# Softmax denominators in a windowed-attention feed-forward: a copy between SBUF tensors in place of a trip through DRAM, and another order of tasks

## What is computed

```
x = x + 0.5 * ffn(layernorm(x))
x = x + attn(layernorm(x))
x = x + 0.5 * ffn(layernorm(x))
```

```
for l in range(2):
    q, k, v = split(shift_token(x) @ wqkv[l])           # 8 heads of 64
    q = l2norm(q) * q_scale[l];  k = l2norm(k) * k_scale[l]
    q, k = rotary_xpos(q, k)
    o = softmax(mask(8 * q @ k.T)) @ v                  # own window and the one before
    x = x + o @ wo[l]
    h = layernorm(shift_token(x)) * ln_g[l] + ln_b[l]
    a, g = split(h @ w1[l] + b1[l])
    x = x + (a * gelu(g)) @ w2[l] + b2[l]
```

## Time and profile before

| | us |
|---|---|
| median of 3 runs | 2139.76 (2129.42 to 2140.91) |
| the profiled execution: its own time | 2146.62 |
| its span, from the first to the last instruction | 2144.8 |
| TensorE busy | 1746.9 (81%) |
| VectorE busy | 1369.1 (64%) |
| GpSimd busy | 979.3 (46%) |
| ScalarE busy | 938.8 (44%) |

### The profile page before, as it was taken

One profiled execution on the slowest core, in us unless ns is written; L12 is line 12 of the kernel. 1 busy time (PEld: TensorE's weight loads), 2 busy tenths in 40 slices (PEclk: granted clock), 3 DMA queues, 4 the chain that ended last, 5 costly groups with the idle time before them and its releaser, 6 DMA issues. The chain is left out here.

```text
span 2144.8 us, 48275 instructions
## 1 busy us (share of the span) xinstructions
PE 1746.9 (81%) x19914; PEld 1024.5 (48%) x19914; DVE 1369.1 (64%) x2002; ACT 938.8 (44%) x1503; POOL 979.3 (46%) x692
## 2 busy tenths in 40 slices
PE   1578888888888887799999997678888888888885
PEld 1345444545545544455555553344444555555543
DVE  2466777666776664456666654577777776666752
ACT  1134444544445443245555554234444544544532
POOL 2444455455455451444444441445445545445530
PEclk9888999999999999589999998799999999999998
DMA  4333343455343452000000000243444534355441
GB/s 143 37 58 63 68 73 64 74 77 86 63 78 63 79 75 50 12 1 2 1 2 1 1 1 1 37 73 63 64 77 73 86 65 76 63 85 86 85 78 36
DMA packets 66060, 118.94 MB, mean 55 GB/s; under 512 B 13183, under 2 KB 23603, under 8 KB 63667
## 3 DMA queue, kind: packets, MB, share of 16 engines
q1 hardware_dynamic: 65843, 115.85, 32.1%
HBM read 49.61 MB, written 3.28 MB: 25 GB/s over the span
## 5 line engine op out<-in xcount | busy, mean ns | idle before, releaser
L953 POOL TENSOR_TENSOR QK<-QK,RB 128x1024 f32<-128x1024 f32 x128 | 302.2, 2361 | 120.2 <-DMA RB<-RN 120.2
L793 DVE SCALAR_TENSOR_TENSOR TP<-banks,cols,tab 128x1024 f32<-128x1024 f32 x256 | 318.3, 1274 | 52.5 <-PE banks L457 46.5
L947 POOL TENSOR_TENSOR QK<-TP 128x512 f32<-128x512 f32 x128 | 164.7, 1287 | 332.0 <-DVE TP L793 288.8
L1315 DVE TENSOR_REDUCE NM<-banks 128x2 f32<-128x1024 f32 (+3 forms) x256 | 202.9, 820 | 129.4 <-PE banks L1128 129.4
L1244 ACT ACTIVATE PTL<-banks 128x1024 f32<-128x1024 f32 (+1 forms) x192 | 168.1, 884 | 192.9 <-PE banks L1159 190.5
L816 DVE TRANSPOSE_TENSOR_REDUCE MX<-banks 128x16 f32<-128x512 f32 x256 | 160.2, 682 | 122.3 <-PE banks L494 122.3
L649 ACT ACTIVATE SQ<-banks 128x512 f32<-128x512 f32 x128 | 76.6, 599 | 279.1 <-PE banks L457 278.8
L834 DVE TENSOR_TENSOR OT<-banks,OT 128x512 f32<-128x512 f32 x128 | 85.3, 687 | 158.6 <-DMA OT<-sums_d 143.9
L939 POOL TENSOR_TENSOR HTL<-Z,HTH 128x512 fp32r<-128x512 f32 x32 | 37.8, 1182 | 303.8 <-ACT HTH L643 303.8
L457 PE MATMUL banks<-HTH,wqkv_h 128*128 128x512 f32 x256 | 125.3, 490 | 54.4 <-DVE TP L793 43.2
L655 ACT ACTIVATE SQ<-banks 128x512 f32<-128x512 f32 x128 | 76.7, 599 | 200.3 <-DVE TP L793 200.3
(11 more groups left out here) (182 smaller groups left out, 3636.0 us busy)
## 6 DMA issues: line engine op xcount, KB each, us to landing
RB<-RN SPq DMA_DIRECT2D x512, 64.0 KB, 4.0
OT<-sums_d SPq DMA_DIRECT2D x128, 256.0 KB, 4.0
V<-V SPq DMA_DIRECT2D x32, 512.0 KB, 6.0
V<-V SPq DMA_DIRECT2D x32, 384.0 KB, 7.1
RB<-vars_d SPq DMA_DIRECT2D x32, 256.0 KB, 3.3
X<-in_L_attn_x SPq DMA_DIRECT2D x8, 256.0 KB, 4.5
out<-X SPq DMA_DIRECT2D x8, 256.0 KB, 4.6
wqkv_raw<-in_L_ffn_wqkv SPq DMA_DIRECT2D x1, 1536.0 KB
```

What stands on the lines that cost most here:

```text
L793: nc.vector.scalar_tensor_tensor(out=TP[:, o:o + 2, :], in0=BK[4 + z][:, :].unsqueeze(1).to_broadcast([P, 2, T]), scalar=q, in1=tab[:, e, ...
L947: nc.gpsimd.tensor_tensor(QK[:, m, 0, :], TP[:, 2, :], TP[:, 1, :], ALU.subtract)
L953: nc.gpsimd.tensor_tensor(QK[:, m, :, :], QK[:, m, :, :], RB[:, m, :].unsqueeze(1).to_broadcast([P, 2, T]), ALU.mult).then_inc(S["nr_ok"], 1)
L1315: last = nc.vector.tensor_reduce(NM[:, G % 2, i, 24 + 32 * h0:57 + 32 * h0:32], PAIR[at(m) % RING][:, :, o:o + (i + 1) * P], AX_X, ALU.max ...
```

## The change

- `sums` on SyncE no longer goes through DRAM. `DR` holds the reciprocal sums of each head in 32 equal rows; for each of two slices j of the group and each quarter of 32 rows, one transfer copies 32 rows of `DR` to 32 rows of `OT`. That makes 8 transfers of 64 KB for each group, where there was one of 8 KB and two of 256 KB. `sums_d` is gone.
- `DR` has two halves, one for each group. ScalarE waits, before it overwrites a half, for the copies of the unit before.
- Every slice j of `OT` has its own semaphore (`d_in0` to `d_in3`), and `attended` j waits for its own.
- `NT_`, VectorE's scratch in `norms`, lies in `RB[:, 3]` now, so VectorE waits until GpSimd has used that slice for the unit before.
- The lists of `run` lines are new on all engines. The loops also begin at another place, which changes the number beside `n` in many lines and not the order around the loop. Counted around the loop, SyncE's order is as before. On TensorE `values` 0 now stands ahead of `attend` 3, `hidden` 1 1 behind `project` 0, `project` 1 ahead of `variance`, and `hidden` 0 0 behind `turn_max` 0; several tasks have other banks, `values` 3 among them, which is in bank 4 behind `attend` 2. On ScalarE `high_hidden` stands ahead of the last square, and squares of m=1 around the second gate. On VectorE `rotate` 1 1 stands ahead of `add_eps`, and `gated` 0 behind `spread_max` 0. On GpSimd `low_hidden` stands ahead of `rotate` 3, and `norms` 0 ahead of `low`.

```diff
-        sums_d = nc.dram_tensor("sums_d", (2, LG, T), F32).ap()
...
-                DR = sb("DR", [P, T])
+                DR = sb("DR", [P, 2, T])
...
                         def sums(u, g):
-                            n = 2 * u + g
-                            sp.wait_ge(S["dl_ok"], n + 1)
-                            sp.dma_start(sums_d[n % 2], DR[0:P:32, :]).then_inc(S["d_out"], 16)
-                            sp.wait_ge(S["d_out"], 16 * (n + 1))
+                            sp.wait_ge(S["dl_ok"], 2 * u + g + 1)
                             if u >= 1:
                                 sp.wait_ge(S["wo_in"], u)
-                            for e in range(2):
-                                src = sums_d[n % 2].rearrange("(j e) n -> e j n", e=2)[e]
-                                sp.dma_start(OT[W * e:W * e + W, 2 * g:2 * g + 2, :],
-                                             src.unsqueeze(0).broadcast_to([W, 2, T])).then_inc(S[("d0_in", "d1_in")[g]], 16)
+                            for j in range(2):
+                                for r in range(0, P, 32):
+                                    h = 2 * j + r // W
+                                    sp.dma_start(OT[r:r + 32, 2 * g + j, :],
+                                                 DR[32 * h:32 * h + 32, g, :]).then_inc(S[f"d_in{2 * g + j}"], 16)
...
                         def sums(u, g, k):
                             n = 2 * u + g
                             act.wait_ge(S["dd_in"], n + 1)
-                            if n >= 1:
-                                act.wait_ge(S["d_out"], 16 * n)
-                            nc.scalar.activation(DR[:, :], BK[k][:, :], ACT.Ln).then_inc(S["dn_ok"], 1)
+                            if u >= 1:
+                                act.wait_ge(S[f"d_in{2 * g}"], 64 * u)
+                                act.wait_ge(S[f"d_in{2 * g + 1}"], 64 * u)
+                            nc.scalar.activation(DR[:, g, :], BK[k][:, :], ACT.Ln).then_inc(S["dn_ok"], 1)
...
                         def norms(u):
                             dve.wait_ge(S["rl_ok"], u + 1)
+                            if u >= 1:
+                                dve.wait_ge(S["nr_ok"], 4 * u)
+                            NT_ = RB[:, 3, :]
...
-                            run(norms, n - 2, 0)
-                            run(norms, n - 2, 1)
...
+                            run(norms, n - 1, 0)
+                            run(low, n)
+                            run(norms, n - 1, 1)
```

More of the change, by code:

```diff
@@ L425, in _ @@
                             run(values, n - 1)
+                            run(variances, n - 2)
+                            run(sums, n - 1, 0)
                         if store:
@@ L589, in _ @@
                         for n in range(-3, NU + 4):
[L590 to L599, removed]
                             run(add_max, n - 2, 1)
-                            run(norms, n - 1, 6)
-                            run(attend, n - 2, 0, 5)
+                            run(norms, n - 1, 7)
+                            run(attend, n - 2, 0, 6)
                             run(sums, n - 2, 1, 4)
@@ L622, in _ @@
                             run(turn_max, n - 1, 0, 7)
+                            run(hidden, n - 3, 0, 0, 6)
+                            run(add_max, n - 1, 0)
+                            run(hidden, n - 3, 0, 1, 7)
+                            run(hidden, n - 3, 0, 2, 6)
+                            run(project, n, 2)
+                            run(scores, n - 1, 1)
+                            run(sums, n - 1, 0, 7)
+                            run(project, n, 3)
+                            run(turn_max, n - 1, 1, 7)
+                            run(outward, n - 3, 6)
                     @block.scalar
@@ L924, in _ @@
                             run(gated, n - 3, 1, 7)
+                            run(gated, n - 3, 2, 6)
+                            run(rotate, n, 2, 1)
+                            run(rotate, n, 2, 0)
+                            run(maxima, n - 1, 1)
+                            run(statistics, n + 1)
+                            run(rotate, n, 3, 1)
+                            run(spread_max, n - 1, 1, 7)
+                            run(rotate, n, 3, 0)
+                            run(outward, n - 3, 6)
+                            run(tokens, n + 1)
+                            run(clamp, n, 7)
+                            run(attended, n - 1, 0, 6)
+                            run(norms, n)
+                            run(attended, n - 1, 1, 6)
+                            run(back, n - 3, 7)
+                            run(arrive, n + 1, 7)
+                            run(attended, n - 1, 2, 4)
+                            run(attended, n - 1, 3, 5)
+                            run(residual, n - 1, 7)
                     @block.gpsimd
@@ L971, in _ @@
                         for n in range(-3, NU + 4):
[L972 to L983 removed]
+                            run(rotate, n - 1, 2)
+                            run(hidden, n - 3)
+                            run(tokens, n)
+                            run(low_hidden, n - 3)
+                            run(rotate, n - 1, 3)
+                            run(norms, n - 1, 0)
+                            run(low, n)
+                            run(norms, n - 1, 1)
+                            run(norms, n - 1, 2)
+                            run(rotate, n, 0)
+                            run(norms, n - 1, 3)
+                            run(rotate, n, 1)
                 stack.pop()
```

96 lines of the change are left out of this document (32 added, 64 removed).

## The result

| | before | after |
|---|---|---|
| median, us | 2140.34 (4 runs of the comparison) | 2216.74 (2211.01 to 2220.78, 4 runs) |
| ratio to before | 1 | 1.0365 [1.032, 1.041] |
| the profiled execution: its own time | 2146.62 | 2211.01 |
| its span | 2144.8 | 2209.2 |
| mean granted TensorE clock over the span | 0.945 | 0.930 |

The changed kernel is slower by 76.4 us. The forecast was 75 us slower.

The account below looks back on a forecast made before the run. A loop of waits through SyncE's queue ahead of the norms bounds it; 30 x (1.5 + 0.75 - 0.6) = 50, plus 3 and 22 for the clock, make 75 on 2139.76: 2215 us. 8 in 10 range: 2118 to 2272.

Parts of the forecast that it names:

- Step 1: SyncE's queue between Exp and norms: eight copies in place of a store and two loads, +1.5 us a unit.
- the first end: SyncE's copies: their data keep up with the issues, m=0's norms come at +11.2 us, +0.95 a unit.
- the second end: SyncE's copies: their data move at 90 GB/s, m=0's norms come at +11.95 us, +1.7 a unit.
- The third end: SyncE's copies: a long issue holds SyncE 6.1 us, norms take as long as before, +13.2, +3.0 a unit.
- Step 2: GpSimd's order: `low` between the norms of m=0 and m=1 makes the scores start later, +0.75 us a unit.
- Step 3: VectorE between scores and rotate 2: `CB` no longer meets GpSimd's m=3, gated 0 is added, -0.6 us a unit.
- Step 4: TensorE ahead of `project` 0: after standing 2.4 to 3.1 us its clock falls in half the units, +22 us in all.
- the main case: The forecast itself, 2215 us, slower through SyncE's copies and TensorE's clock; range given as 2174 to 2247, chance 0.60.
- The throttle: Rival on SyncE: the copies hold its queue 6.1 us and the norms come no quicker, 2282 us, chance 0.13.
- The cheap queue: Rival on SyncE: copies issue at 0.37 us with the gap, m=0's norms come 1.15 earlier, 2110 us, chance 0.16.
- The order pays for the copies: Rival: VectorE's two variance products come free beside GpSimd's rotate 1, about 1.0 us each, 2133 us, chance 0.11.

Follow-up runs that it names:

- the copies' experiments: Copies alone in the order of before, 2256.05 us; and the changed kernel with 16 copies of 32 KB a group, 2347.59, or four of 128 KB, 2563.36.
- with the hop: The changed kernel's new order, with the sums again going through DRAM by a store and two loads in place of the copies: 2120.3 us, ratio 0.9919.
- the filler: The changed kernel plus 14 useless matmuls on TensorE between the join and `project` 0 in each unit but the first two: 2178.49 us, ratio 1.0181.

## Why the prediction was right

**What bounds the kernel: right.** The loop through SyncE's queue ahead of the norms was the place, and an `OT` that lands earlier brought nothing by itself (the join starts 0.5 us earlier in the changed kernel, and TensorE stands longer behind it). Both the copies' experiments and the kernel without a transfer for group 1 say so: whatever lengthens SyncE's work between Exp and norms lengthens the unit, whatever takes it away shortens it.

**Step 1: +1.5 predicted, +1.88 measured; the sum's value was right and its base was not.** m=0 was to come at +11.75 and came at +11.84. But the +10.25 of before was read from one unit; the mean is 9.96. Of the ends, the first had the mechanism: data that keep up. Its 6.15 behind the issues were 6.20, and the landing in 2.0 us, with the DMA engines 0.32 busy, speaks against the second end, data at 90 GB/s. What the first end lacked was a long issue among the eight in many units: SyncE is held 5.6 us and not 5.05. The third end foresaw such an issue, at 6.1, but not that the norms then come quicker than before.

The Trainium skill's figures (DMA: Bandwidth & Descriptors, section Measured) gave an estimate of 3.8 us for the eight copies' data, less than their issues; the figures are for loads from DRAM that GpSimd issues, not for copies between SBUF tensors. The trace agrees that the data are not the limit (5.6 us of issues, DMA engines 0.32 busy). The price of smaller transfers shows here in the issues alone: 32 KB and 64 KB land in the same 2.0 us.

**Step 2: +0.75 predicted; +0.48 measured up to the scores, and nothing at the maxima.** The working held (GpSimd's second product, then the scores), and the measured size is a third less than the one taken: 5.4 and 6.15 behind m=0 were taken, the means are 5.54 and, with the hop, 6.03 (by the weight load of the first mask). The term was then taken as a loss for the unit. With the hop it was paid by the clock: the scores, released without a stand, no longer met the low clock that cost 0.45 a unit before. I had counted the clock only as a loss of the changed kernel and not asked what it already took.

**Step 3: -0.6 predicted, -0.53 measured (-0.42 with the hop).** The leg of this step runs from the scores to VectorE's rotate 2, and behind rotate 2 VectorE takes the maxima of group 1. The windows from the maxima of group 0 to those of group 1, before and after (columns as in the earlier trace rows; VectorE is the third engine), show it busy for all but 0.4 us:

```profile
486.36:500.70 14.34, 11.85 (x176) 7.09 (x176) 13.94 (x17) 8.39 (x15) 7.42 (x5) 1.00 0.26 67
```

```profile
501.79:515.62 13.83, 12.60 (x179) 7.57 (x179) 13.47 (x18) 8.17 (x15) 7.44 (x5) 1.00 0.05 17
```

So VectorE's own work sets this leg, and a shorter task in it shortens the unit. `CB` went from 2.11 to 0.99 us in the mean, -1.12 where I took -1.42, and gated 0 put some 0.6 into the leg where I took 0.75. GpSimd is not quite through with m=3 when `CB` starts: its product from 504.42 to 506.78 overlaps the `CB` at 506.34 by 0.44 us, and the one before by 1.56. Without an overlap `CB` took 0.68; beside this product it took 0.54 plus the overlap, 0.98 and 2.10.

**Step 4: +22 us predicted, 38 measured by the filler.** The mechanism was right, in place too: `project` 0 was to start at +15.4 and started at +15.36, at the low clock. The term was mis-sized, at 0.73 us a unit where it took 1.25: I charged half of the units, because I let the join end at +12.3 to +13. It ended earlier (+11.5 in the unit at 478 us), since the copies land in 2.0 us and not in 4.0; so TensorE stands 3.6 us on average and not 2.4 to 3.1, and nearly every unit pays, most of them in full.

So all four steps had the right place, and steps 3 and 4 the right mechanism as well. Step 1's +1.5 was chosen nearer to an end that did not happen, and step 2 left out the low clock of before that it did away with. That the sum was right to 2 us is in part luck, since errors of size cancel: per unit step 1 and the clock cost some 0.4 and 0.5 more than I counted, step 3 brought a little less, and step 2, 0.75 in the sum, cost nothing at the maxima. The sign rested on step 1, which held. (Worked out again from its terms, the range of the main case is 2176 to 2243, not 2174 to 2247; nothing hangs on it.)

**The rivals.** The throttle (SyncE held 6.1 and the norms no quicker) did not happen: 5.6, and 6.20 behind it. The cheap queue needed less than 0.49 an issue; no copy was under 0.507. The order pays for the copies in part, by 20 us of 96 to 115, and not where that rival looked, in VectorE's variance products (1.29 and 1.26 us in both kernels), but where step 3 did.

The Trainium skill says (DMA: Bandwidth & Descriptors, section Issuing engines are not separate DMA queues) that the sequencer's time to start a DMA is usually small beside the DMA. Here it is not: 0.59 us of issue stand against 2.0 us to landing, they add up for eight, and half the bytes cost the same issue.

## What to carry to other kernels

Count the issues that stand in a queue ahead of the transfer on which the loop waits, at their measured price each, before counting bytes: replacing three transfers by eight small ones cost 2 us a unit here, though the eight landed faster. When a stall ahead of TensorE grows, look which of its work comes right behind the stall, and whether that is on the loop; and ask what the low clock already costs there before the change. A mean over all units, from one fixed event, shows which leg pays; a total of waits and a single unit both misled here. Cut the legs where the loop runs: between the two groups' maxima that is VectorE, and a leg that ends at TensorE's `add_max` would put the gain of `CB` in the wrong place.

## What the runs showed of the hardware

- Issue time did not depend on size between 32 and 64 KB: 0.589 and 0.591 us in the median. Now and then one takes longer, up to 1.97 us; among eight copies of the changed kernel that is one over 0.9 us in 17 of 28 units.
- A copy of 64 KB from 32 rows to 32 rows landed in 2.0 us, a transfer of 64 KB from one row to 32 rows in 4.0, and one of 128 KB from one row to 64 rows in 12.3, with issues that took up to 6.4 us.
- A higher mean clock was no gain by itself: 0.932 and 0.946 with the hop, at equal spans (2124.2 and 2124.6). With the copies, 0.930 and 0.945 were worth 38 us. What counts is whether the work at the low clock is on the loop.
- A second stand moved the low clock. With sixteen copies TensorE stood ahead of the join too, the clock was low over the join, and it was at its full level again for `project` 0 and the scores, which gave back 1.26 us a unit.
- A VectorE instruction that took 0.68 us alone (`CB`, 64x512) took 0.54 us plus the time for which GpSimd's product with the norms (L953) ran beside it: 0.98 us at 0.44 of overlap, 2.10 at 1.56.
